# One key block for two heads, column-tiled scores in odd units, and a new order on SyncE

## The reference

```
xn  = layernorm(x)
ctx = xn @ We.T;  influence = ctx @ ctx.T            # 16 context features
scores = (Q @ K.T) * SCALE + 0.1 * influence         # per head, 256 x 256
out = softmax(scores) @ V @ Wo.T                     # 16 heads of 8 features
top2 of softmax(xn @ gate_w.T); y = sum p * (gelu(xn @ w1[e] + b1[e]) @ w2[e] + b2[e])
x + out + y
```

## Time and profile before

| | |
|---|---|
| median of 3 runs | 708.39 us (707.06 to 710.24) |
| the profiled execution | 708.61 us, its span 706.9 us |
| TensorE busy | 648.2 us, 92% |
| VectorE busy | 614.9 us, 87% |
| ScalarE busy | 541.7 us, 77% |
| GpSimd busy | 467.7 us, 66% |
| mean granted TensorE clock | 0.982 of 2.4 GHz |

### The profile page before, as it was taken

How to read it: one execution, slowest core, us unless ns; L and a number is a source line. 1 busy time by engine, 2 the same in 40 slices (tenths; PEclk the granted TensorE clock), 3 DMA queues, 4 the chain that set the end, 5 groups by cost and what they waited for, 6 DMA issues and landing times.

```text
span 706.9 us, 24553 instructions
## 1 busy us (share of the span) xinstructions
PE 648.2 (92%) x7800; PEld 431.8 (61%) x7800; DVE 614.9 (87%) x1106; ACT 541.7 (77%) x1123; POOL 467.7 (66%) x542
## 2 busy tenths in 40 slices
PE   0367799999999999989999999999999999999997
PEld 0264345555555555579999999998455555555454
DVE  8979789999899999868888888888999999999991
ACT  2583378888888888778888888888778878778775
POOL 8680468676687767226656656656687878878774
PEclk9996799999999999999999999999999999999999
DMA  9859656866766757684555554553667778677752
GB/s 246 316 159 320 166 135 170 207 166 180 198 165 178 208 167 176 164 129 100 101 106 99 108 100 100 106 101 72 154 160 189 177 189 184 170 183 192 170 121 80
DMA packets 162947, 113.32 MB, mean 160 GB/s; under 512 B 72624, under 2 KB 150448, under 8 KB 162864
## 3 DMA queue, kind: packets, MB, share of 16 engines
q1 hardware_dynamic: 153632, 90.63, 52.7%
q0 software_dynamic: 8192, 16.86, 9.7%
q10 hardware_dynamic: 1040, 4.76, 1.8%
HBM read 55.42 MB, written 47.19 MB: 145 GB/s over the span
## 4 chain that ended last, share of the span: by engine, by line
PE 62%; DVE 20%; issue 6%; SPq 5%; DMA 3%; ACT 2%; ACTq 0%; DVEq 0%
PE bank L1267 13%; PE mx L1256 13%; PE bank L1140 12%; DVE mx L960 11%; PE bank L1118 10%; PE mx L1152 6%; PE bank L1038 2%; DMA stack<-qk_dram 2%; DVE A L795 2%; DVE mT L966 2%; PE bank L1202 2%; DVE lo_qk L980 1%; ACT A L712 1%; PE bank L1169 1%; SPq L318 1%
## 5 line engine op out<-in xcount | busy, mean ns | idle before, releaser
L712 ACT ACTIVATE A<-bank 128x512 f32<-128x512 f32 x502 | 278.4, 597 | 62.9 <-PE bank L1140 53.9
L960 DVE TENSOR_REDUCE mx<-mx 128x4 f16<-128x1024 f32 x256 | 302.8, 1205 | 20.6 <-PE mx L1152 11.6
L583 POOL TENSOR_SCALAR rows<-rows,slot_p 128x128 f32<-128x128 f32 x142 | 112.1, 799 | 95.7 <-DVE rows L1015 95.6
L1140 PE MATMUL bank<-stack 113*128 113x256 f16 x1004 | 171.4, 277 | 1.4 <-ACT A L712 0.6
L569 POOL DMA_INDIRECT slots_x<-rows,pos x128 | 123.7, 966 | 53.0 <-PE bank L1140 32.6
L613 POOL DMA_INDIRECT rows<-slots_y,pos x128 | 121.4, 948 | 39.7 <-PE bank L1140 18.3
L1118 PE MATMUL bank<-A,V 128*32 128x256 f32 x2048 | 137.1, 385 | 1.3 <-ACT A L712 1.3
L756 ACT ACTIVATE rows<-mx,b 128x256 f32<-128x256 f32 x284 | 111.7, 475 | 25.5 <-PE mx L1256 23.7
L1140 PEld LDWEIGHTS bank<-stack 113*128 113x128 f16 x1004 | 72.7, 98 | 90.1 <-ACT A L712 55.0
L1007 DVE TENSOR_TENSOR rows<-rows 128x512 f16<-128x512 f32 x142 | 101.4, 715 | 25.0 <-ACT rows L760 22.5
L1267 PE MATMUL bank<-w,rows 128*128 x1704 | 106.9, 219 | 1.3 <-DVE rows L1007 1.3
(11 more groups left out here) (142 smaller groups left out, 595.2 us busy)
## 6 DMA issues: line engine op xcount, KB each, us to landing
stack<-ctx_rest SPq DMA_DIRECT2D x64, 256.0 KB
stack<-qk_dram SPq DMA_DIRECT2D x128, 96.0 KB
slots_y<-rows SPq DMA_DIRECT2D x71, 128.0 KB, 2.1
qk_dram<-hi_qk SPq DMA_DIRECT2D x64, 128.0 KB
stack<-ctx_high SPq DMA_DIRECT2D x128, 64.0 KB
slots_x<-A ACTq DMA_DIRECT2D x1, 4644.0 KB, 20.0
w_stage<-in_w SPq DMA_DIRECT2D x8, 512.0 KB
qk_dram<-lo_qk SPq DMA_DIRECT2D x64, 64.0 KB
```

What stands on the lines that cost most here:

```text
L583: ins = pool.tensor_scalar(ye[n % 4][:, h, :], ye[n % 4][:, h, :], slot_p[:, n // 4 % 3, n % 4, h:h + 1], None, ALU.mult)
L712: act.activation(A[:, n % NA, :, :].rearrange("p h s -> p (h s)"), scores(k, n)[:, :], ACT.Exp, scale=SCALE).then_inc(s_xp, 1)
L960: dve.tensor_reduce(mx[:, a, 8 * qt:8 * qt + 8].rearrange("q (i e w) -> q i e w", i=2, e=2)[:, :, g % 2], MX[u % 2][:, :].rearrange("q (i ...
L1140: mm = pe.matmul(scores(k, n)[:, i * S:(i + 1) * S], stack[0:SHIFT + 1, par, h, 1, c * P:(c + 1) * P], stack[0:SHIFT + 1, par, h, 0, :], s ...
```

## The change

The stack has six blocks of four heads a batch in place of 32 head blocks: four query blocks, and two key blocks each of which holds the keys of two heads, one in each class of rows. A score product then has one set of weights (128 keys, or 32) and 512 moving columns (both heads' queries). In even units it is one matmul; in odd units four column tiles of 32 keys. The small products stand in even units after both scores: project at u = 0, the value projection at u = 2, the transposes of O at u = 4, of o_n at u = 6; the output, now in column tiles, at u = 7 between the two scores. ScalarE's and VectorE's parts move with them, and VectorE adds to x at the head of u = 0.

The maxima of a half are turned with two transposes of 64 x 32; shift_rows still has two transfers, now of pieces of 32 elements. A load has six transfers a half (ctx_rest in two), write has three. SyncE runs write first in an iteration, then the stores, then the loads and shift rows; in the prologue it loads batch 1 ahead of contexts 1 to 3, and ScalarE's queue takes the rest of the clearing. The context parts get a tile of their own, and GpSimd's first scatter comes four units later.

```diff
-START = 4
+START = 8
-        stack = sb("stack", [P, 2, H, 2, S], F16)
+        stack = sb("stack", [P, 2, 6, 4, S], F16)
+        part_c = sb("part_c", [P, 4, 2, 2 * S], F16)
-        mT = sb("mT", [32, 2, 2, P], F16)
+        mT = sb("mT", [64, 2, 2, 2, 32], F16)
+        def q_side(par, h):
+            return stack[:, par, h // 4, h % 4, :]
+        def k_side(par, h):
+            return stack[:, par, 4 + h // 8, h % 4, :]
...
             def load(half2, par2, g):
-                sp.dma_start(stack[REST:REST + 2 * DE, par2, 8 * g:8 * g + 8, :, :], rest).then_inc(s_st[par2][g], 16)
+                sp.dma_start(dst, rest[:, :, 0:S].to_broadcast([2 * DE, 8, S])).then_inc(s_st[par2][g], 16)
+                sp.dma_start(stack[REST:REST + 2 * DE, par2, 4 + g, :, :], rest[:, :, S:2 * S].to_broadcast([2 * DE, 4, S])).then_inc(s_st[par2][g], 16)
...
             def shift_rows(a, b1_, par1):
-                for c in range(2):
-                    sp.dma_start(stack[SHIFT:SHIFT + 1, par1, 8 * a:8 * a + 8, 0, c * P:(c + 1) * P], mT[8 * c:8 * c + 8, par1, a, :]).then_inc(s_mr[par1][a], 16)
+                rows_ = stack[SHIFT:SHIFT + 1, par1, 2 * a:2 * a + 2, :, :].rearrange("r b w (c j i q) -> r (b w c) j i q", c=2, j=2, i=2)
+                for i in range(2):
+                    sp.dma_start(rows_[:, :, :, i, :], mT[32 * i:32 * i + H, par1, a, :, :]).then_inc(s_mr[par1][a], 16)
...
+            def write_ahead(k, b3_, par3, half3):
+                if k is None or b3_ >= 2:
+                    for h in range(2):
+                        sp.wait_ge(s_st[par3][h], n_st)
+                write(par3, n_hq, n_lq)
             def attend(s, f, k, first_half=True):
+                if f["p"] and k != -1:
+                    write_ahead(k, b3_, par3, half3)
+                if k == 0:
+                    context(3)
+                if not first_half and f["c"]:
+                    store_rows(s, k)
...
-                            for i in range(4):
-                                ins = dve.transpose(mT[:, par1, a, 32 * i:32 * i + 32], mx[32 * i:32 * i + 32, a, :])
+                            for j in range(2):
+                                ins = dve.transpose(mT[:, par1, a, j, :], mx[64 * j:64 * j + 64, a, :])
...
                     def shifted(p):
-                        for i in range(2):
-                            h = 8 * (g // 2) + 4 * p + 2 * (g % 2) + i
-                            mm = pe.matmul(scores(k, n)[:, i * S:(i + 1) * S], stack[0:SHIFT + 1, par, h, 1, c * P:(c + 1) * P], stack[0:SHIFT + 1, par, h, 0, :], start=True, stop=True)
+                        h, w = 8 * (g // 2), 2 * (g % 2) + p
+                        m = 32 if u % 2 else P
+                        for j in range(0, P, m):
+                            mm = pe.matmul(scores(k, n)[j:j + m, :], k_side(par, h + w)[0:SHIFT + 1, c * P + j:c * P + j + m], stack[0:SHIFT + 1, par, h // 4:h // 4 + 2, w, :], start=True, stop=True)
...
+                    def output():
+                        drained(7, s, f, k)
+                        for q in range(2):
+                            for j in range(0, P, 32):
+                                mm = pe.matmul(MISC[j:j + 32, S + q * P:S + (q + 1) * P], oT[:, q * P + j:q * P + j + 32], wo[:, :], start=True, stop=True)
                     for p in range(2):
                         if f["x"] and not (opening and u == 0):
                             shifted(p)
-                        if p == 0:
-                            small_products()
+                        if u == 7 and p == 0 and f["o"] and k != B - 1:
+                            output()
+                    small_products()
```

More of the change, by code:

```diff
@@ L240, in scores, with both_sides @@
             return ring[n % len(ring)] if k == B - 1 else EX[n % 2]
+        def q_side(par, h):
+            return stack[:, par, h // 4, h % 4, :]
+        def k_side(par, h):
+            return stack[:, par, 4 + h // 8, h % 4, :]
+        def both_sides(row, n, par, g, i):
+            first_, second_ = 2 * g + i, 4 + g
+            return stack[row:row + n, par, first_:second_ + 1:second_ - first_, :, :]
         def head_values(par, c, g, i):
@@ L342, in write @@
+                sp.dma_start(bass.AP(q.tensor, q.offset, [[S, P], [5 * part, 2], [1, S]]), hi_qk[:, :, :]).then_inc(s_wr[par3], 16)
                 sp.wait_ge(s_lq, n_lq)
-                for side in range(2):
-                    sp.dma_start(bass.AP(q.tensor, q.offset + (S if side else 2 * part), [[2 * S, P], [1, S]]), lo_qk[:, side, :]).then_inc(s_wr[par3], 16)
+                sp.dma_start(bass.AP(q.tensor, q.offset + 2 * part, [[S, P], [part, 2], [1, S]]), lo_qk[:, :, :]).then_inc(s_wr[par3], 16)
@@ L396, in attend @@
                         sp.dma_start(b2, B2.to_broadcast([P, NE * D])).then_inc(s_b2, 16)
+                    if k == -1:
+                        if g == 0:
+                            for h in range(2):
+                                load(half2, par2, h)
+                        shift_rows(g, b1_, par1)
+                        if g == 0:
+                            write_ahead(k, b3_, par3, half3)
+                        context(g + 1)
+                        continue
+                    if k == 1 and g == 1:
+                        for r in range(1, 4):
+                            sp.wait_ge(s_cw[r], 96)
                     if f["l"]:
-                        if k is None or k >= 0:
-                            sp.wait_ge(s_ex, 16 * b + 8 * g + 8)
+                        sp.wait_ge(s_ex, 16 * b + 8 * g + 8)
                         load(half2, par2, g)
@@ L402, in attend @@
                         shift_rows(g, b1_, par1)
[L403 to L408, removed]
                 c = low_chunk(s, k, first_half)
@@ L557, in _ @@
             places(0, Tb)
-            pool.wait_ge(s_zero, 64)
+            pool.wait_ge(s_zero, 48)
             pool.wait_ge(s_prob, 1)
@@ L1156, in small_products @@
                     def small_products():
-                        if u == 3 and f["m"]:
-                            drained(3, s, f, k)
+                        if u == (1 if opening else 0) and f["p"]:
+                            drained(0, s, f, k)
+                            if k == 0:
+                                pe.wait_ge(s_cntr, 2)
+                            if k == 1:
+                                pe.wait_ge(s_routed, 2)
+                            project(b3_)
+                        if u == 2 and f["m"]:
+                            drained(2, s, f, k)
                             for q in range(2):
@@ L1198, in attend @@
                         values(bo, paro, 3)
-                    def output():
-                        for q in range(2):
-                            mm = pe.matmul(MISC[:, S + q * P:S + (q + 1) * P], oT[:, q * P:(q + 1) * P], wo[:, :], start=True, stop=True)
-                        mm.then_inc(s_wo, 1)
-                    if u == 0 and f["c"] and k != B:
-                        drained(0, s, f, k)
-                        output()
                     if u == 0 and f["o"] and not closing:
                         values(bo, paro, 3)
-                    if u == 1 and opening:
-                        pe.wait_ge(s_fy, ET)
-                    if u == 1 and f["p"]:
-                        drained(1, s, f, k)
-                        if k == 0:
-                            pe.wait_ge(s_cntr, 2)
-                        if k == 1:
-                            pe.wait_ge(s_routed, 2)
-                        project(b3_)
                     if u in ((3, 5, 7) if k == B - 1 else (2, 4, 6)) and f["x"]:
```

140 lines of the change are left out of this document (65 added, 75 removed).

## The result

The changed kernel takes **718.2 us** in the median (715.95 to 723.41, four runs) against 708.7 of the kernel before in the same session: ratio 1.016, 95% interval 1.013 to 1.020 (the two medians alone give 1.013). The forecast was 712.4, in a range of 695 to 723: the direction and the range held, the size did not. The profiled execution took 715.95 us.

What follows compares the result with a forecast made beforehand. The prediction took VectorE and TensorE to hold each other, with ScalarE close. 27 iterations at +0.25 us (+6.8) and the prologue's -3.0 gave +3.8 on 708.61, so 712.4 us, range 695 to 723.

Steps and rivals of the forecast that it cites:

- the wait at the banks: TensorE's second even score product waits for ScalarE's exp at two score banks, units 2, 4, 6: +1.01 us an iteration.
- the gains: Savings an iteration from fewer tile-shape switches (-0.40), small products and output (-0.10), and TensorE's waits for VectorE (-0.26): -0.76 us.
- The switches: Tile-shape changes on TensorE, three a lap in place of four, 0.10 each over four laps: -0.40 us an iteration.
- The sum of an iteration: All terms of one iteration together: -0.40 - 0.10 - 0.26 + 1.01 = +0.25 us, over 27 iterations +6.8.
- the transposes: Two a half in place of four on VectorE; TensorE's two waits for VectorE go: -0.26 us an iteration.
- V's product and the output: Small products in even units and attention output as column tiles on TensorE: -0.10 us an iteration, 0 to -0.2.
- late loads: SyncE's new order makes the next load late by under 1 us, second half only; taken as 0.
- a rival with a chance of 0.10: Loads or shift rows land late on SyncE: 27 x 0.35 us on top, 722 us; chance 0.10.
- The prologue: Batch 1's load goes ahead of contexts 1 to 3, so TensorE's 3.68 us wait shrinks: -3.0 us, 0 to -3.7.

Runs made afterwards that it cites:

- both remedies: Changed kernel with small products of even units between their two scores and SyncE's loop in the order of the kernel before: 695.1 us, 0.983.
- the last experiment: Kernel before with only SyncE's loop order of the changed kernel put in (write first, then stores, then loads and shift rows): 727.6 us, 1.031.

## Why the prediction was right in direction and short in size

**The direction: right by luck.** Slower was forecast because in each iteration the wait at the banks (+1.01) outweighed the gains (-0.76). With SyncE's loop in its former order, which leaves that balance and the new prologue as they are, the kernel takes 706.8 us, 0.999 (0.998 to 1.000) of before. So it was not that balance that made the change slower. It was SyncE's order, for which the sum had 0.

**The wait at the banks: right in place and length.** Forecast were odd scores 0.88 after the values and the second even product 1.57 (unit 4) and 1.67 (units 2 and 6) after the odd pair, none at unit 0; measured are 0.89, 1.58, 1.74 and 1.66, and none at unit 0. The page TensorEngine Tiling (Array Packing), PSUM Bottleneck, of the Trainium skill warns that the emptying of PSUM may bind once tiles quicken TensorE. The trace agrees in that the scores wait for ScalarE, though ScalarE is busy for only 18.97 us of 25, but the tiles are not what made it bind: without them an iteration is no shorter (13.57 against 13.39).

**The switches: right in size each, about half of it in an iteration.** Full scores behind column-tiled values come 0.11 later. The Trainium skill, in TensorEngine Tiling (Array Packing), Key Properties, says that a change of mode drains the engine; the trace agrees, with this 0.11. Of the -0.40 an iteration, undoing the tiles gave back 0.18 and 0.20 in the changed kernel and 0.21 in the first half with both remedies. No median shows it: 718.2 and 720.0, 695.1 and 695.5 lie within the intervals.

**The sum of an iteration: too large.** +0.25 us, 6.8 in all, was forecast. With the loads in time (SyncE's loop in its former order) the first half stands at 13.39 against 13.37, the last fourteen iterations at 13.28 against 13.18, and iteration 16 has 0.9 more: 12 x 0.02 + 14 x 0.10 + 0.9 = 2.5. Both sides of the sum came out at about half. The wait: the new place of the small products takes 13.39 to 12.89 and 13.28 to 12.79, half a microsecond where 1.01 was in the sum; the weight loads of the maxima products then wait 12.8 us in 145 for VectorE, in place of 8.9. The gains: these iterations lie 0.48 and 0.39 under those of before, where 0.76 was in the sum (12.45 was forecast without the wait). Of them, one key block and two transposes alone, without the new order, gave 0.13 and 0.10 (13.24 and 13.08); -0.26 was counted for the transposes. What V's product and the output gave was not taken apart.

**SyncE: the step that failed.** The text took 0 for late loads, and kept +9.5 as a rival with a chance of 0.10, because it counted the write's wait for lo_qk and five issues and found the load late by under 1 us. It left out the write's other wait, for the landing of both loads that read the block it overwrites: 0.97 us of SyncE's idle time at 593.4, 8.7 us in 145. Moving the order back returned 11.4 us of the medians, more than the whole loss of 9.5. By the profiled executions it returned 8.6, of which 3.9 lie in the last fourteen iterations and 4.6 ahead of iteration 3, where one execution says little (next paragraph). In the other two versions the order costs more: the last fourteen iterations take 13.66 against 12.79 with the small products between the scores, 13.93 against 13.08 without the new order of products. That the write's place is the larger part is shown by moving it alone; how much of it is the landing, how much its three issues in front of the load, was not separated. The smaller pieces of the shift row, which that rival named too, are not the cause: they stay when the order goes back, and TensorE then waits for a shift row once between 515 and 660 us, for 0.9.

**The prologue: -3.0 was forecast, and single executions do not show it.** The wait of 3.68 went, and with SyncE's loop order of before iteration 3 starts at 120.5 in place of 124.0. But the kernel of the last experiment has the prologue of before up to iteration 0, and in its execution the maxima products that waited 3.68 hardly wait (their weight loads 0.59, in the trace of before 4.0):

```profile
79.52 0.33 PEld L1161 LDWEIGHTS mx<-stack 64*128 64x128 f16 x8 [0.59 <-DMA stack<-qk_dram]
```

There iteration 3 starts at 121.0. So the gain may be 3.5 us or 0.5. In the changed kernel iteration 3 starts at 125.1, and the wait for the load of batch 2 alone does not make that: with full matmuls TensorE waited 3.07 at this place, with the write moved back 2.88, and iteration 3 started at 121.3 and 120.5. What sets the changed kernel's execution apart is the granted clock behind the wait (last section), and so up to 3.8 of the 4.6 us that the former order seems to return ahead of iteration 3 need not be the order's. It is context(3) in front of the load that makes most of the wait: with context(3) moved behind the load and the write left in front, the weight loads wait 0.45 there.

So two errors met: the iteration's sum was 4 us too high, and SyncE's part some 11 us too low (0 against 11.4 by the medians); 712.4 - 4 + 11 = 719, near the 718.2 measured.

## What to carry to other kernels

An in-order queue of transfers is a resource like an engine: when an item moves to its head, list every semaphore that it waits for (its buffer's last readers too, not only its data) and the slack of each transfer behind it. Where two limits lie close, an experiment that takes away one shows the other (4 us for the order of the products, 11 for SyncE, 23 for both), so try them together before calling either worthless. And keep independent work between two products that share a pair of banks: put behind them, the same work no longer fills the wait.

## What the runs showed that was not expected

- Column tiles cost the same as the full matmul when it is the shape that its neighbour has: an odd pair is followed by the maxima products after 0.55 us in tiles (580.16 to 580.71) and 0.54 as full matmuls (592.91 to 593.45 on the timeline of the version without tiles). What they save is the switch alone.
- A wait of TensorE for a load was followed by a lower granted clock in one execution and not in another. In the changed kernel it waited 3.27 us, and from 94 to 98 us the clock was 0.50 of 2.4 GHz, the level of 1.2. With full matmuls it waited 3.07 at the same place and kept 1.00. The changed kernel, then the version with full matmuls (92 to 100 us):

```profile
92.00:100.00 8.00, 6.55 (x49) 2.80 (x49) 3.28 (x4) 3.00 (x6) 1.94 (x2) 0.57 0.46 133
```

```profile
92.94 0.61 PE L1176 MATMUL mx<-stack 64*128 64x256 f16 x8 [3.07 <-DMA stack<-qk_dram]
92.00:100.00 8.00, 6.97 (x76) 3.22 (x76) 5.95 (x8) 4.98 (x11) 3.60 (x4) 1.00 0.50 145
```

  With the small products between the even scores it waited 4.22, had 0.79 in this stretch, and started iteration 3 at 123.3. With both remedies the stretch ran at 1.00, TensorE busy for 7.96 us of 8. So in these executions a later start of iteration 3 goes with the lower clock, by up to 4 us; that the clock alone makes it was not shown. A change of the prologue has to be judged by more than one execution.
